# Square products in tiles 1 to 7: all matmuls with high parts of one product in a row, then all with low parts, or the other way round

## The reference, cut to what matters

```python
xn = _layernorm(x)                                  # x: 8 x 1024 rows of 256
s  = random-feature attention of xn                 # two 256-wide products and exponentials
h = silu(tlin(xn, w1)) * tlin(xn, w2)               # 256 -> 1024, ternary weights, a scale per output
h = gelu(tlin(h, h1))                               # 1024 -> 1024  (square layer 0)
h = gelu(tlin(h, h2))                               # 1024 -> 1024  (square layer 1)
g = silu(tlin(h, w3))                               # 1024 -> 256
out = x + s * g
```

## Time and profile before

| what | value |
|---|---|
| median of three runs | 1252.62 us |
| the profiled execution's own time | 1251.94 us |
| its span (first to last instruction) | 1250.1 us |
| PE busy | 1241.9 us, 99% of the span |
| DVE, ACT, POOL busy | 1034.5 us (83%), 934.4 us (75%), 281.4 us (23%) |
| granted TensorE clock | 0.998 of full speed |

### The profile page before, as it was taken

How to read it: one execution, slowest core, us unless ns; L and a number is a source line. 1 busy time by engine, 2 the same in 40 slices (tenths; PEclk the granted TensorE clock), 3 DMA queues, 4 the chain that set the end, 5 groups by cost and what they waited for, 6 DMA issues and landing times.

```text
span 1250.1 us, 16620 instructions
## 1 busy us (share of the span) xinstructions
PE 1241.9 (99%) x5976; PEld 820.6 (66%) x5976; DVE 1034.5 (83%) x1427; ACT 934.4 (75%) x1426; POOL 281.4 (23%) x325
## 2 busy tenths in 40 slices
PE   9999999999999999999999999999999999999997
PEld 7666676666766666666666666666676666766666
DVE  8889889887898888978888888888888888887775
ACT  5466767778677796778878778787787877787664
POOL 7985122030220302203022030220303112040000
PEclk9999999999999999999999999999999999999999
DMA  9689942575234851358414483145831557315441
GB/s 342 247 315 300 346 162 84 170 216 191 91 102 157 245 179 68 109 178 243 153 68 143 144 267 129 68 144 167 253 119 68 172 157 245 108 52 168 148 147 36
DMA packets 97352, 209.49 MB, mean 168 GB/s; under 512 B 13424, under 2 KB 16624, under 8 KB 96240
## 3 DMA queue, kind: packets, MB, share of 16 engines
q1 hardware_dynamic: 80032, 156.98, 38.2%
q0 software_dynamic: 17232, 51.39, 13.1%
HBM read 175.78 MB, written 38.83 MB: 172 GB/s over the span
## 4 chain that ended last, share of the span: by engine, by line
PE 99%; DVE 1%; ACT 0%; issue 0%; POOL 0%; POOLq 0%
PE ps L1010 64%; PE ps L938 12%; PE ps L1072 9%; PE ps L965 4%; PE ps L847 4%; PE ps L1045 0%; PE ps L1042 0%; PE ps L1034 0%; PE ps L1031 0%; PE ps L1026 0%; PE ps L1038 0%; PE ps L1023 0%; PE ps L1089 0%; PE ps L885 0%; DVE rows L1904 0%; PE ps L891 0%
## 5 line engine op out<-in xcount | busy, mean ns | idle before, releaser
L1010 PE MATMUL ps<-split_hi,ring 128*128 128x512 f32 x1792 | 453.6, 404 | 0.0
L1010 PE MATMUL ps<-split_lo,ring 128*128 128x512 f16 x1792 | 406.3, 380 | 0.0
L1010 PEld LDWEIGHTS ps<-split_hi,ring 128*128 128x128 f32 x1792 | 336.7, 188 | 82.6 <-DMA ring<-in_h 0.8
L1690 DVE SCALAR_TENSOR_TENSOR split_lo<-quad,split_hi 128x1024 f16<-128x1024 f32 x224 | 281.6, 1268 | 108.4 <-ACT split_hi L1238 108.3
L1010 PEld LDWEIGHTS ps<-split_lo,ring 128*128 128x128 bf16 x1792 | 166.5, 98 | 214.2 <-issue 27.5
L1238 ACT ACTIVATE split_hi<-quad 128x1024 fp32r<-128x1024 f32 x224 | 232.5, 1049 | 43.0 <-PE ps L1010 31.9
L1282 ACT ACTIVATE quad<-quad,cols_s 128x512 f32<-128x512 f32 x192 | 136.5, 719 | 50.0 <-DVE quad L1724 23.0
L1716 DVE TENSOR_TENSOR quad<-quad 128x1024 f32<-128x1024 f32 x128 | 161.4, 1289 | 0.7
L661 POOL TENSOR_TENSOR quad<-quad,s 128x256 f32<-128x256 f32 x56 | 45.5, 840 | 413.1 <-ACT quad L1274 413.1
L645 POOL DMA_DIRECT2D z_h<-xin x56 | 55.6, 1000 | 154.2 <-DVE xin L1547 154.2
L1290 ACT ACTIVATE quad<-ps 128x512 f32<-128x512 f32 x64 | 38.2, 597 | 36.1 <-PE ps L1010 36.1
(11 more groups left out here) (212 smaller groups left out, 1839.9 us busy)
## 6 DMA issues: line engine op xcount, KB each, us to landing
ring<-hs SPq DMA_DIRECT2D x428, 256.0 KB, 3.8
xin<-in_x SPq DMA_DIRECT2D x16, 512.0 KB, 4.2
s_h<-s SPq DMA_DIRECT2D x16, 512.0 KB, 4.2
seen<-in_h POOLq DMA_DIRECT2D x32, 256.0 KB, 4.4
res<-in_x SPq DMA_DIRECT2D x15, 512.0 KB, 4.9
out<-res SPq DMA_DIRECT2D x15, 512.0 KB, 2.6
z_h<-xin POOLq DMA_DIRECT2D x56, 128.0 KB, 6.2
xT_hi<-z_h POOLq DMA_DIRECT2D x14, 512.0 KB, 7.0
```

The lines of the kernel that those rows point to most:

```text
L1010: mm = e.matmul(ps[:, 4 * (w % 2) + m, :], weights, moving, start=first and k == 0 and begins, stop=last and k == Q - 1 and not begins, sk ...
L1690: e.scalar_tensor_tensor(out=both(slots_lo[i], g), in0=both(quad[at[t][L][FAST[w][1]]], g), scalar=POWER[L], in1=both(slots_hi[i], g).bitc ...
```

## The change

In tile 0 and in products 1.0 and 1.3 of every tile ("woven") the order stays as it was. In all others of tiles 1 to 7 all 16 matmuls of one kind come first, m0 to m3, then the 16 of the other. Low comes first in products 0.0, 0.2, 0.4, 0.6, 1.2, 1.5; high comes first in 0.1, 0.3, 0.5, 1.1, 1.4, 1.6. Only TensorE's order is changed; ACT's, DVE's and the DMA queues' programs are as they were. In the new order an m's first matmul is number 0, 4, 8, 12 (before: 0, 4, 16, 20), and `prod` is raised after 19, 23, 27, 31 (before: 11, 15, 27, 31).

```diff
+LOW_FIRST = [(0, 0), (0, 2), (0, 4), (0, 6), (1, 2), (1, 5)]
+WOVEN = [(1, 0), (1, 3)]
@@ product(t, L, w)
-                for m, g in [(m, g) for two, parts in ((0, (0, 1)), (2, (1, 0))) for g in parts for m in (two, two + 1)]:
-                    begins = g == m // 2
+                if t == 0 or (L, w) in WOVEN:
+                    turns = [(m, g) for two, parts in ((0, (0, 1)), (2, (1, 0))) for g in parts for m in (two, two + 1)]
+                else:
+                    begin = int((L, w) in LOW_FIRST)
+                    turns = [(m, g) for g in (begin, 1 - begin) for m in range(Q)]
+                for i, (m, g) in enumerate(turns):
+                    begins = all(v != m for v, _ in turns[:i])
                     if begins:
                         bank_free(t, L, w, m)
                     if g:
```

## The result

The changed kernel takes 1291.59 us (median of five runs, 1288.39 to 1294.51) against 1252.62 us before: a ratio of 1.0316, 95% interval 1.0302 to 1.0329. It is 39 us slower. I had forecast 1286.5 us, range 1276 to 1295. The profiled execution took 1294.51 us; its span is 42.4 us longer than before.

A forecast was written before the change was run, and what follows sets the result against it. TensorE was taken to run without a gap, bound by its matmuls' spacing. Tiles 1 to 6 at 5.05 us each (30.3) plus tile 7's 3.9 gave 34.2 us on 1251.94, predicted as 1286.5 us, range 1276 to 1295.

The forecast's parts named there:

- place C: Product 1.5: PE waits for the low half at its start and DVE's addition of m3 at matmul 12, 2.25 us.
- place A: Product 0.5, matmul 12: PE waits for DVE's addition of 0.4's m3, 2.8 us late in tiles 1 to 6.
- place B: Start of product 1.4: its first matmul waits for ACT's two high halves, 0.3 us late.
- fewer changes of kind: Square layers: 5 to 6 fewer pairs of switches between hi and lo matmuls, saving 0.3 us a tile.
- tile 7, A and C: Tile 7, products 0.5 and 1.5: waits at matmul 12 for the addition of m3, 2.1 us each.
- full clock throughout: PE: the granted clock stays full, as no single expected pause is over 2 us.
- the clock: Rival, 2%: pauses lower the clock, ten matmuls at 1.2 GHz after each of A and C, 30 us: 1316 us.
- a granted clock under 1: Sign named in advance that would make the prediction wrong.
- floor rival: Rival, 6%: the later m0 does not carry through to m3, only the earlier waits cost: 1261 us.
- not-slower rival: Rival, 4%: hi matmuls in runs of 32 reach the lo spacing, 17 us saved: 1246 us; includes both near zero.
- advice on rotating through the banks: Skill's rule: matmul groups rotate through PSUM banks while ACT and DVE empty one; against the new order, no figure.
- rule on weight loads pulled ahead: Skill's rule: PE may pull weight loads past waits, restarts up to 0.1 us cheaper each, 4 us in all: 1282.

The follow-up runs named there:

- only_04_05: The kernel before with the new order in products 0.4 (low first) and 0.5 (high first) alone: 1274.75 us (1.0181).
- w05: The changed kernel with product 0.5 woven as before, its m3 beginning at matmul 20 again: 1278.67 us (1.0223).
- w04: The changed kernel with product 0.4 woven as before, its m0 ready after matmul 11 again: 1275.97 us (1.0191).
- rows_later: The changed kernel with six small layer-norm operations on DVE moved from before 0.4's addition of m3 to product 0.5, m = 2: 1283.57 us (1.0251).
- rows_more: The changed kernel with twelve in place of six small layer-norm operations on DVE before 0.4's addition of m3: 1306.44 us (1.0431).
- halves_first: The changed kernel with both halves of the next product's high (ACT) and low (DVE) parts ahead of block m0's work, tiles 1 to 7: 1272.91 us (1.0160).
- only_14_15: The kernel before with the new order in products 1.4 (high first) and 1.5 (low first) alone: 1266.77 us (1.0127).
- runs8: The kernel before with runs of 8 in place of 16 matmuls of a kind in tiles 1 to 7: 1256.83 us (1.0035).
- only_01_02: The kernel before with the new order in products 0.1 (high first) and 0.2 (low first) alone: 1252.50 us (1.0002).
- end_16: The changed kernel with product 1.6 woven in tile 7 alone: 1292.07 us in one run.

## Why the prediction was right, step by step

A first matmul of a run of hi after lo (or after the mix) is recorded 0.19 us early (in tile 3 the first hi matmul after place C starts 0.03 us after its predecessor and 0.42 us before its successor, against 0.22 and 0.23 expected), so a tile that now begins with lo and ends before hi reads 0.38 us less against its old value than it took, half of it at each end; I count by distances between starts.

| step | forecast | measured | shown by |
|---|---|---|---|
| place A, tiles 1 to 6 | 2.8 us | 2.84 us in tile 3 | only_04_05, w05, w04, rows_later, rows_more |
| place B | 0.3 us | 0.34 us | trace; goes with halves_first |
| place C | 2.25 us | 2.14 us | only_14_15 |
| fewer changes of kind | 0.3 us | 0.37 us | trace; runs8 and only_01_02 for a pair |
| tile 7, A and C | 4.2 us | 4.16 us | trace |
| tile 7, before `down` | none | 1.15 us | trace, end_16 |
| full clock throughout | yes | falls after A in 3 of 6 tiles, 1.3 to 1.6 us each | trace, rows_more |

The forecast was right in its mechanism and in the size of each place: the later m0 moved the queues by 1.68 us, they carried it through to m3, and PE asked earlier. Only the shape at A was other than I had it: pauses of 0.7 us at matmul 8 and 1.8 at matmul 12, and a restart of 0.11 us at each of matmuls 4, 8 and 12, in place of one pause. The sum is nearly the same, since the addition of m3 ends the last pause in either case.

The net of a tile is 2.84 + 0.34 + 2.14 - 0.37 = 4.95 us, forecast 5.05. The profiled run's 42.6 us over the run before are then: six tiles 29.7, falls of the clock about 4.6, tile 7 4.9, and the rest, some 3, mostly in the start and tile 0, whose program is the same (waits for DMA that differ from run to run; the median run is 2.9 us faster).

The profiled run is 42.6 us over the run before, and my sum had 34.2. Two terms that it did not have are 5.8 us of the 8.4 us between them, and the start and tile 0 are most of the rest. The first is the clock. I had it as a rival at 2%, with ten matmuls at 1.2 GHz behind every pause of A and C, 30 us. It came true in part: only behind the longest pause, in half of the tiles, 4.6 us. The reason that I gave against it, a first slice at full clock in spite of 1.5 us without work, says little about a pause of 1.8 us. I had also written that a granted clock under 1 would make the prediction wrong. It fell in short stretches only: 0.994 over the span against 0.998, and the row of slices stays at 9. The second is the 1.15 us before `down`. It was missed because I worked the chains only as far as the squares' own products; behind a later m0 stand the GELUs of b21 as well. How many falls a run gets differs: the five runs, with clocks of 0.993 to 0.997, lie 6 us apart. That the median came no further from the forecast is in part luck.

The floor rival (1261 us) is out: it needed slack in DVE's queue, and none was there. The not-slower rival is out too: the changed kernel's run of 32 hi matmuls behind place C gives (7.65 - 0.39 - 0.19) / 31 = 0.228 us, and no drop to the lo spacing. The Trainium skill's advice on rotating through the banks ("Perfetto Trace Analysis", Matmuls) went the way of the result. Its rule on weight loads pulled ahead ("TensorE: Matmul & The Clock Gate", Part 1) gave 1282 us. In tile 3 the loads were held up by the waits: PE started 0.05 to 0.06 us after the end of the instruction that it waited for. The next matmul came 0.11 us later than usual at each restart with hi matmuls (A and B), and on time at the two restarts with lo matmuls (C).

## What to carry to other kernels

When the consumer's order changes, take each wait twice: how much earlier it is asked, and how much later its producers get their input; the two add up where the queue between has no idle time. What stands behind a block in an in-order queue moves with it, so the producers' queues have to be reordered together with TensorE's: the same order of matmuls cost 39 us with the old queues and 20.5 with two halves moved, and a part of it with fitting queues was 1.4 us faster than before. A longer run of one kind is worth about 0.05 us for each pair of changes saved, so a single wait of 1 us eats twenty of them.

## What the runs showed of the hardware that I had not expected

- The granted clock. Behind a pause of PE of 1.8 us (one of 0.7 us ends 1.0 us before it) the clock fell to 1.2 GHz in 3 of 6 tiles of the changed kernel, in 4 of 6 of end_16 and in 2 of 6 of only_04_05; behind 3.0 us in 6 of 6 of rows_more. Behind 1.6 us and less (halves_first, only_14_15, w05, w04, rows_later) no profile shows a fall. (Of w05's other three runs one took 1284.09 us at a mean clock of 0.997, the others 0.998; what happened in it no trace shows.) A fall lasts for 6 to 14 matmuls, and it starts at once or up to four matmuls behind the pause. The page "TensorE: Matmul & The Clock Gate" of the Trainium skill says (Part 1) that the clock has these two levels and that idleness brings the lower one; the traces agree, with 0.50 of full speed in the row of tile 4. It is not the tile: the changed kernel and end_16, with the same program in these tiles, fell in different ones. What does decide, these runs do not show.
- Hi matmuls after lo need about ten matmuls to come down to their settled distance of 0.227 us, from up to 0.236; lo matmuls are at 0.216 from the second on (changed kernel, tile 3, products 1.5 and 1.6).
